# Two masked-attention steps and part of the expert sum move to GpSimd and ScalarE

## The reference, cut to what matters

```python
x = x + tanh(g_xattn[0]) * xattn0(ln(x), ctx)          # 16 heads of 16
x = x + tanh(g_ffn[0])   * experts0(ln(x))             # top 2 of 8 experts
x = x + tanh(g_xattn[1]) * xattn1(ln(x), ctx, mask)    # biases; scores clipped to +-100, masked keys -inf
x = x + tanh(g_ffn[1])   * experts1(ln(x))             # top 2 of 8 experts
x = x + tanh(g_xattn[2]) * xattn2(ctx, ln(x))          # biases
x = x + tanh(g_ffn[2])   * dense_experts(ln(x))
x = x + tanh(g_xattn[3]) * one_head(ln(x), ctx)
x = x + tanh(g_ffn[3])   * fp4_ffn(ln(x))
# experts: gates = softmax(x @ gate_w + gate_b); the two largest, times (x @ expert_w[e] + expert_b[e]), summed
# attention: softmax(q k^T / 4) v, with q = x wq + bq, k = ctx wk + bk; then @ wo + bo
```

## Time and profile before

| | us |
|---|---|
| median of 3 runs | 1721.33 (1719.80 to 1724.51) |
| profiled execution | 1719.49 |
| its span, first to last instruction | 1717.7 |
| PE busy | 1455.6 (85%) |
| DVE busy | 1227.8 (71%) |
| ACT busy | 649.9 (38%) |
| POOL busy | 252.5 (15%) |
| granted PE clock, mean | 0.942 of 2.4 GHz |

### The profile page before, as it was taken

One profiled execution on the slowest core, in us unless ns is written; L12 is line 12 of the kernel. 1 busy time (PEld: TensorE's weight loads), 2 busy tenths in 40 slices (PEclk: granted clock), 3 DMA queues, 4 the chain that ended last, 5 costly groups with the idle time before them and its releaser, 6 DMA issues. The chain is left out here.

```text
span 1717.7 us, 39505 instructions
## 1 busy us (share of the span) xinstructions
PE 1455.6 (85%) x12076; PEld 1021.2 (59%) x12076; DVE 1227.8 (71%) x4062; ACT 649.9 (38%) x1531; POOL 252.5 (15%) x350
## 2 busy tenths in 40 slices
PE   1899999699768888888779959999997998968887
PEld 1677777455346666665445436777765886854554
DVE  6577676488758888888478846666654884659995
ACT  2466666411124444444321116555552223321111
POOL 1223233000012222222000003223230000000000
PEclk9799999799889999999789969999998998989999
DMA  3543433200032222222000043222315342310000
GB/s 105 155 103 90 102 95 79 70 6 0 1 91 68 66 65 62 62 65 52 1 26 0 0 123 84 72 77 69 77 41 151 118 141 59 106 42 6 11 11 17
DMA packets 175972, 110.23 MB, mean 64 GB/s; under 512 B 80809, under 2 KB 172972, under 8 KB 175276
## 3 DMA queue, kind: packets, MB, share of 16 engines
q1 hardware_dynamic: 175900, 109.32, 23.8%
HBM read 83.47 MB, written 25.77 MB: 64 GB/s over the span
## 5 line engine op out<-in xcount | busy, mean ns | idle before, releaser
L625 ACT ACTIVATE p<-ps 125x448 f32<-125x448 f32 x576 | 309.3, 543 | 271.9 <-PE ps L906 140.6
L761 DVE TENSOR_REDUCE negm<-ps 112x1 f32<-112x375 f32 x512 | 261.3, 542 | 84.6 <-PE ps L878 83.1
L878 PE MATMUL ps<-kst,qst 96*112 96x375 f16 x768 | 239.3, 347 | 35.7 <-DMA qst<-q_split 24.0
L893 PE MATMUL ps<-qst,kst 112*125 112x224 f16 (+1 forms) x1152 | 212.1, 267 | 5.0 <-POOL qst L600 3.2
L1217 PE MATMUL ps<-fw,xs_e 128*112 128x512 f16 x768 | 186.3, 387 | 0.0
L600 POOL TENSOR_TENSOR qst<-m_row,diag 16x448 f16<-16x448 f16 x128 | 128.2, 1029 | 331.9 <-ACT m_row L666 331.9
L893 PEld LDWEIGHTS ps<-qst,kst 112*125 112x125 f16 (+1 forms) x1152 | 146.3, 138 | 46.5 <-issue 17.7
L917 PE MATMUL ps<-p,v 125*32 125x112 f32 x4608 | 153.0, 266 | 1.0 <-ACT p L625 1.0
L878 PEld LDWEIGHTS ps<-kst,qst 96*112 96x112 f16 x768 | 97.5, 131 | 92.5 <-DVE negm L761 35.9
L757 DVE CUSTOM_DVE_ANT_0 with_mask<-ps,mask_add 112x375 f16<-112x375 f32 x256 | 135.2, 546 | 22.0 <-issue 22.0
L743 DVE TENSOR_SCALAR ps<-ps 125x448 f32<-125x448 f32 x192 | 120.3, 626 | 37.9 <-PE ps L893 37.9
(11 more groups left out here) (215 smaller groups left out, 2205.3 us busy)
## 6 DMA issues: line engine op xcount, KB each, us to landing
kst<-k_split SPq DMA_DIRECT2D x288, 93.8 KB, 2.3
k_split<-ks SPq DMA_DIRECT2D x48, 375.0 KB, 3.5
fw<-in_w SPq DMA_DIRECT2D x16, 1024.0 KB, 6.9
qst<-q_split SPq DMA_DIRECT2D x576, 14.0 KB, 1.8
stage<-in_ctxT SPq DMA_DIRECT2D x16, 375.0 KB, 3.7
ctxn<-in_ctx SPq DMA_DIRECT2D x16, 375.0 KB
q_split<-qs SPq DMA_DIRECT2D x48, 112.0 KB, 2.0
fw<-in_ew SPq DMA_DIRECT2D x2, 2048.0 KB, 7.7
```

What stands on the lines that cost most here:

```text
L625: act.activation(g.p[hg % 2][:, kt, :], ps[0:KR, BK_ST + s % 2, 0:4 * S], ACT.Exp).then_inc(s_exp, 1)
L761: dve.tensor_reduce(g.negm[1 - par][:, h:h + 1], scored, AX_X, ALU.max, negate=True).then_inc(s_max, 1)
L878: mm = pe.matmul(ps[0:S, BK_S + h % 2, 0:SK], g.q_stack[q][0:96, h, :], g.k_stack[q][0:96, h // 2, :], start=True, stop=True)
L893: mm = pe.matmul(bank[:, 2 * r * S:2 * (r + 1) * S], g.k_stack[par][0:rows, pr, kt * KR:(kt + 1) * KR], g.q_stack[par][0:rows, 2 * pr:2 * ...
```

## The change

- Attention 1 and 2 (`biased`): ACT writes k in single precision to `g.stage`; POOL casts the high part and subtracts for the low part, ahead of its split of q. DVE does neither. Layer 0 keeps both on ACT and DVE.
- Attention 1: POOL makes the mask, behind its four products of the body. ACT normalises the rows, from a table of -mean/deviation, at the end of a body for batch i+3. In the other layers DVE does it at the same place.
- Layers 0 and 2: the turn of the weighed values moves from slot 3 to 4 and the turn back from 5 to 6. Layer 0 scales q in one ACT instruction instead of two.
- The bias products have 128 rows instead of 3 or 8, the added ones zero.
- Experts: ACT scales experts 0 to 3; POOL sums these, and adds the sum to what DVE has made of x, the bias and experts 4 to 7. PE computes the gate logits before its second bank; the turned gate weights have a bank of their own; both maxima and weights stand elsewhere in DVE's order.

```diff
@@ PLANS, layers 0 and 2
-                turn=3, back=5, out=9, stats=[9, 10, 11], q=2, maxima=14, split=12, rows=1, keys=[0, 2]),
+                turn=4, back=6, out=9, stats=[9, 10, 11], q=2, maxima=14, split=12, rows=1, keys=[0, 2]),
@@ attention, gpsimd
+                if biased and on["p"]:
+                    b = i + 2
+                    at_least(pool, s_mstack, (i + 1) * HG)
+                    if clipped:
+                        at_least(pool, s_mask, i + 2)
+                    for m in range(KC):
+                        pool.wait_ge(s_kf, 2 * b + m + 1)
...
+                        carry(pool, g, 1 + m)
+                        pool.tensor_copy(g.k_split[par][:, 0, m, :], g.stage[par][:, m, :]).then_inc(s_khi, 1)
+                        pool.wait_ge(s_khi, 2 * b + m + 1)
+                        pool.tensor_tensor(g.k_split[par][:, 1, m, :], g.stage[par][:, m, :],
+                                           g.k_split[par][:, 0, m, :], ALU.subtract).then_inc(s_klo, 1)
                 if on["p"]:
...              (split of q)
                 if on["m"]:
...              (four products, m_stack)
+                if clipped and on["p"]:
+                    pool.wait_ge(s_maskin[par], 16 * (turn.half(2) + 1))
+                    at_least(pool, s_mstack, (i + 2) * HG)
+                    at_least(pool, s_st, (i + 1) * ST_SLOTS)
+                    carry(pool, g, 3)
+                    pool.tensor_scalar(g.mask_add[par][:, :], g.mask_in[par][:, :], 0.0, g.far[:, 0:1], ALU.is_equal,
+                                       ALU.mult).then_inc(s_mask, 1)
@@ attention, scalar, end of the body
+                if on["n"] and clipped:
+                    b = i + 3
+                    act.wait_ge(s_shift, 1)
+                    at_least(act, s_t, b - 1)
+                    act.activation(g.xn[1 - par][:, :], g.x[:, b, :], ACT.Identity, scale=g.rstd[:, bass.ds(b, 1)],
+                                   bias=g.shift[:, bass.ds(b, 1)]).then_inc(s_xn, 1)
@@ attention, vector
-                if on["p"]:
-                    b = i + 2
-                    at_least(dve, s_t, b - 1)
-                    normed(dve, g, b, par).then_inc(s_xn, 1)
...
-                if clipped and on["p"]:
-                    dve.wait_ge(s_maskin[par], 16 * (turn.half(2) + 1))
-                    at_least(dve, s_st, (i + 1) * ST_SLOTS)
-                    dve.tensor_scalar(g.mask_add[par][:, :], g.mask_in[par][:, :], 0.0, g.far[:, 0:1], ALU.is_equal,
-                                      ALU.mult).then_inc(s_mask, 1)
+                if on["n"] and not clipped:
+                    b = i + 3
+                    at_least(dve, s_t, b - 1)
+                    normed(dve, g, b, 1 - par).then_inc(s_xn, 1)
@@ experts_top2, gpsimd, one body
+                        at_least(pool, s_x, i)
+                        pool.wait_ge(s_scaled, i * ON_ACT + 2)
+                        pool.tensor_tensor(summed[0][:, :], scaled[0][:, :], scaled[1][:, :], ALU.add)
...              (+ scaled[2], + scaled[3])
+                        pool.wait_ge(s_acc, i + 1)
+                        pool.wait_ge(s_summed, i * 3 + 3)
+                        pool.tensor_tensor(g.x[:, i, :], summed[0][:, :], acc[par][:, :], ALU.add).then_inc(s_x, 1)
@@ experts_top2, vector: order of one body after the change
+  logits(i+1); statistics of batch i-1, first part (waits s_x, i); maximum(i+1); normed(i+2); statistics, second part
+  top value(i+1) (waits for the exponential); statistics, third part; expert 4; top index; bias; reciprocal
+  expert 5; weights w(i+1); low half of the turned rows (i+2); experts 6 and 7
@@ experts_top2, tensor: order of one body after the change
+  experts bank 0; logits(i+1); bank 1; turn of w(i); bank 2; bias product; bank 3; turned rows (i+2)
```

## The result

Before 1721.88 us (median of 4 runs beside the others), after 1766.64 (1764.4 to 1768.81, 4 runs): ratio 1.0259, 95% interval 1.0239 to 1.0279. The change makes the kernel 45 us slower. I had said 1715 and a range up to 1737, so the result lies outside it. The profiled execution took 1764.40, with a span of 1762.6.

The account below looks back on a forecast made before the run. PE was taken to hold layers 0 and 2, a PE-DVE loop the experts, a PE-DVE ping-pong masked attention. Terms 27.0, -24, -3.4, -6.4 and +0.3 gave -6.5 us: 1719.5 to 1713, as median 1715, range 1696 to 1737.

Parts of the forecast that it names:

- the order: Masked attention: POOL's mask queues behind four products, so DVE's first masked maximum starts at 612.80 and not at 609.50.
- the mask's 0.60: Masked attention: POOL's mask of 375 columns priced from its cast at 0.60 us, bounds 0.42 and 1.02.
- rival (1): Masked attention: POOL's mask is slow, each 0.1 us costing 1.5; 1736 with a 2 us conversion; chance 0.17.
- A clock drop in masked attention's new 2 us waits: Masked attention: excluded from the rivals, as the last stage had clock 1.00 with PE busy 81.66 of 97 us.
- 1.85 forecast: Masked attention: delay per body from waiting for POOL's mask, in 15 bodies +27.7 us, bounds +25 to +34.
- the normalisation on ACT: Masked attention: row normalisation reaches PE 0.6 us later but hides behind the new wait; without it up to 9 us.
- rival (3): Masked attention makes up its delay, as DVE loses 2.05 us of work per body: layer +5, kernel 1693; chance 0.18.
- 6.4 forecast for both: Experts, two layers: bodies of 6.4 us instead of 7.25, bounds 6.27 and 6.9, -24 us for both layers.
- rival (2): Experts: the loop through POOL holds them; at 6.9 us per body the gain falls to about 9, kernel 1730; chance 0.20.
- layer 1's count: Sum for layer 1's attention, +27.0 us, said to include layer 2's prologue.
- The padding: Output bias products padded with zero rows: saves 0.23 us per body in layers 0 and 2, 0.1 in layer 1.
- The turn: Layers 0 and 2, turn moved from slot 3 to 4: nothing in layer 0, 0.2 us per body in layer 2.

Follow-up runs that it names:

- warm: Changed kernel with eleven idle PE products in front of the second mask product of each masked body: 1736.97 us, ratio 1.0105 to the kernel before.
- mask_as_cast: Changed kernel with POOL's mask made by a plain cast at the same place, without comparison and multiplication: 1723.49 us, ratio 1.0019 to the kernel before.
- pool_forms: Changed kernel with eight POOL operations on 128x375 added one after another at the start, to time each form: 1767.78 us, one run.
- mask_on_dve: Changed kernel with only layer 1's mask back on DVE, at the end of the body: 1689.54 us, ratio 0.9829 to the kernel before.
- mask_xn_dve: Changed kernel with layer 1's mask and row normalisation both back on DVE: 1672.98 us, ratio 0.9721 to the kernel before.
- third_mask_xn: `mask_xn_dve` with POOL's third addition in the experts waiting for DVE's gate weights: 1667.65 us, ratio 0.9674 to the kernel before.
- den_reduce: `mask_xn_dve` with DVE's sum of the top two in layer 1's experts taken by a reduction: 1666.84 us, one run.
- best: Changed kernel, POOL's mask before the products, normalisation on DVE, third expert addition behind the weights, layer 0's turn at slot 3: 1666.32 us, ratio 0.9687.
- mask_first: Changed kernel with POOL's mask of layer 1 moved in front of the body's four products: 1692.88 us, ratio 0.9838 to the kernel before.

## Why the prediction was wrong

**Right: the order.** The mask stands behind four products, DVE's first masked maximum waits for it, and behind that the clip for which PE waits. I put the maximum at 612.80 where the products start at 607.84, so 4.96 later. It is 5.95 later (643.23 to 649.18): by 0.99 more, of which the mask is 0.97. The second and third mask product were to start 6.19 and 7.50 behind the products' start; they start 7.10 and 8.83.

**Wrong: the mask's 0.60.** I priced it from the cast, "as a one-input operation is nearest to the cast", with 1.02 as the upper end. It took 1.57, past the 1.2 that I had set as the sign of rival (1). The nearest row was the wrong kind: which instruction it is counted, not how many inputs it has. Rival (1) had the mechanism and the price of it (1.5 us for each 0.1); `warm` against `mask_as_cast` is 1.12 per body for 1.07 of mask. I gave it 0.17, since all POOL rows of the attention stayed under 1.1. At my own price the 0.97 is 15 us and the forecast 1730: this error alone would have stayed within my range. The same operation on the same tile takes 1.57 on POOL against 0.418 on DVE, and with one operation alone still 1.16 (`pool_forms`).

**Wrong: the clock, which I ruled out.** "A clock drop in masked attention's new 2 us waits is not among them", from the last stage's PE busy for 81.66 of 97 us at 1.00, which is 84%. Masked attention has 81% and gets 0.88; `mask_as_cast` has 82% over the length of four bodies, at 1.00:

```profile
509.20:603.60 94.40, 77.26 (x803) 53.68 (x802) 66.59 (x276) 44.85 (x97) 34.88 (x61) 1.00 0.25 61
```

So the share over a long stretch is no argument. What `warm` and `mask_on_dve` don't have is the second wait: here two, of 1.32 and 2.53 us, lie within 7 us, and the low clock comes at the end of the second; the last stage has one of 1.65 every 10 us. The low clock costs 2.60 per body (`warm`), the largest term of the miss: with its 29.7 us on top of 1730 the sum is 1759, outside the range.

Per masked body: 22.10 + 1.85 forecast = 23.95; + 0.97 for the mask, + 2.60 for the clock, - 0.20 left over = 27.32. That the remainder is small and below zero fits `mask_as_cast`, which has 23.60 at full clock with a mask shorter than mine by 0.1.

**Wrong by its size: the normalisation on ACT.** I said 0.6 per body if the new wait didn't hide it. It is 1.31 (`mask_xn_dve`). It was hidden in the end, and yet it may have done harm: it is the first of the two waits in front of the clock's fall. Whether the second alone would have done it wasn't tried, so its part in the fall stays open.

**Half seen: DVE's lighter load.** I took nothing for it beyond the second clip's, and rival (3) had it. Without the mask's wait the two splits are worth 0.89 per body, and masked attention reaches 20.69 against 22.10. In the kernel as changed the wait covers that.

**Experts.** 6.4 forecast for both, 6.23 and 6.77 measured; -14.9 and -8.2 us where I had -12 for each. In the second, rival (2)'s "missed meeting" is real: tiny DVE instructions stretched by POOL's additions (the cast from 0.16 to 0.56) make the weights and, behind them in DVE's queue, the low half of the turned rows late, and PE waits for that half in front of its gate products:

```profile
985.41 0.47 PE L1304 MATMUL ps<-gws_e,xs_e 128*112 128x8 f16 x6 [0.26 <-DVE xs_e L1290]
```

What the runs show beside POOL's additions is 0.55 against 0.15 for the cast (`mask_xn_dve`, `third_mask_xn`) and 0.34 against 0.14 for an addition of two tiles (`mask_xn_dve`, before), both ending with POOL's instruction, and 0.135 for a reduction (`den_reduce`). It is otherwise beside POOL's mask in `best`, where a copy takes 0.57 against 0.17 and ends a microsecond before the mask does. Why some are held up and others not, no run shows.

Two slips in my sums are small. By the pace of its own row (1.12 for four, the last one's 0.4 in it) two halves of the bias take 0.48, not 0.44; they take 0.43 to 0.49 in the first experts and 0.52 in the second. And layer 2's prologue, +1, was said to be inside layer 1's count but isn't (27.7 + 0.5 - 1.2 = 27.0), so the sum should have been 1716.

**Layers 0 and 2.** 16.5 and 16.6 forecast, 16.47 and 16.53 measured. The padding was 0.23 (0.1 in layer 1) and is 0.32 in all three; a product of 128 rows lets the next start 0.11 later where it was 0.24, 0.13 of it; where the other 0.19 lies no row shows:

```profile
663.80 0.27 PE L879 MATMUL ps<-bo_rows,ones 128*112 128x256 f16 x1
663.91 1.02 PE L881 MATMUL ps<-wo,oT 128*112 128x256 f32 x4
```

The forecast's 0.107 for 256 columns at 2.4 GHz agrees with the pace of the rows at a granted clock of 1.00: 0.216 for 512 columns, so 0.108 for 256 and 2.37 columns per ns, and 0.11 here. A frequency itself stands in no row.

The turn gives 0.18 in layer 2 (I said 0.2) and costs 0.07 in layer 0 (I said nothing). Of layer 2's 15 x 0.48 = 7.2 us, the stage shows 3.6. The gain is made in 12 intervals only, 5.6 us, and 2.1 are lost at the ends: before POOL's first products 0.4, in the second interval 0.6 (17.61 where it was 17.01), from the last interval on 1.1. Why was not followed; I had put +1 on the prologue.

## What to carry to other kernels

Before an instruction moves to an engine that looks idle, find what stands in that engine's queue in front of it at the moment when its result is wanted: moved by four instructions, the same mask on the same engine made the difference between 2.6% slower and 1.6% faster (`mask_first`). Price it from a row of the same instruction on that engine, and where there is none, measure it by itself first. Where a change makes PE wait twice within a few microseconds, as here 1.32 and 2.53, count its next products at half the clock in a rival at least (here 0.50 for 6.8 us, 2.60 us per body); full clock at the same busy share elsewhere doesn't exclude it.

## What the runs showed of the hardware

- POOL, 128x375: cast 0.50 us, `tensor_scalar` with one operation 1.16, with two 1.49 (1.57 with a value per row). Integer or single-precision input makes no difference to the cast (0.50 for both) and the two-operation forms (1.49 for both, 1.58 and 1.56 with a value per row).
- The granted clock fell to 0.50, for 6.8 us a time, at the end of the second of two waits of 1.32 and 2.5 us with 3.2 us of work between them, in each of bodies 3 to 12; with a second wait of 1.35 to 1.41 us, in 2 of the 10 and for 3.4 us, from 1.1 to 1.4 us behind the wait's end (`mask_as_cast`), and with it filled with work, or with the first alone, in none.
- On one or two columns, DVE's addition of two tiles takes 0.34 us, its cast 0.55 when it starts inside one of POOL's additions, and its copy 0.57 beside POOL's mask; alone they take 0.14, 0.15 and 0.17. A reduction of two columns is not affected (0.135).
- A product of 3 rows in front of one of 128 costs 0.32 us more per body than the same padded with zeros.
